# Six weight lows of the first expert on GpSimd during the choice of experts, six of the second expert's in their place on VectorE

## What is computed

```
logits = xn @ router_w + router_b
top_vals, top_idx = top_k(logits, 2)
h = relu(einsum('td,edh->eth', xf, w1) + b1)
y = einsum('eth,ehd->etd', h, w2) + b2
out = einsum('etd,te->td', y, gating)
x = x + s * silu(out)
```

## Time and profile before

| | |
|---|---|
| median of 3 runs | 1032.6 us (1032.31 to 1035.81) |
| the profiled execution | 1037.49 us, of which 1035.7 us are the span from first to last instruction |
| busy, share of the span | TensorE 94%, VectorE 84%, ScalarE 62%, GpSimd 33% |
| mean granted TensorE clock | 0.995 of full |
| routing and first two experts' lows | about 0 to 83 us |
| expert blocks on TensorE | from 78.4 us |

### The profile page before, as it was taken

One profiled execution on the slowest core, in us unless ns is written; L12 is line 12 of the kernel. 1 busy time (PEld: TensorE's weight loads), 2 busy tenths in 40 slices (PEclk: granted clock), 3 DMA queues, 4 the chain that ended last, 5 costly groups with the idle time before them and its releaser, 6 DMA issues.

```text
span 1035.7 us, 25206 instructions
## 1 busy us (share of the span) xinstructions
PE 978.3 (94%) x8418; PEld 764.4 (74%) x8418; DVE 875.0 (84%) x1707; ACT 646.0 (62%) x1383; POOL 338.6 (33%) x342
## 2 busy tenths in 40 slices
PE   0799999999999899999998999999999999999997
PEld 0667888888889799976666666776766777777786
DVE  7899889887676455659999999999999999999972
ACT  4853333333333243438898988888888888888860
POOL 2017889999996300011010102121212121212111
PEclk9999999999999999999999999999999999999999
DMA  9866776766665523227999999999999999999993
GB/s 284 257 268 156 192 195 181 201 191 185 179 180 168 149 57 63 68 87 151 186 169 183 164 178 176 187 196 169 177 187 180 197 187 182 174 168 172 169 179 99
DMA packets 426749, 178.39 MB, mean 172 GB/s; under 512 B 362714, under 2 KB 416548, under 8 KB 425860
## 3 DMA queue, kind: packets, MB, share of 16 engines
q1 hardware_dynamic: 364644, 131.53, 63.1%
q10 hardware_dynamic: 55504, 27.55, 10.5%
q0 software_dynamic: 6480, 17.70, 7.2%
HBM read 54.42 MB, written 34.60 MB: 86 GB/s over the span
## 4 chain that ended last, share of the span: by engine, by line
PE 37%; DVE 13%; issue 2%; ACT 2%; DMA 1%; ACTq 0%; SPq 0%; DVEq 0%
PE b_psS L1411 11%; PE b_psO L1439 11%; PE b_psJ L1456 6%; PE b_psJ L1370 5%; DVE b_ph L1652 4%; DVE b_nmax L1614 4%; PE b_psS L1467 2%; PE b_psO L1442 1%; DMA b_pT<-b_ph 1%; DVE b_outs L1658 1%; ACT b_pr L1521 1%; DVE b_psJ L1622 1%; DVE b_Q L1636 1%; ACT b_ph L1551 1%; DVE b_f L1664 0%
## 5 line engine op out<-in xcount | busy, mean ns | idle before, releaser
L1054 PE MATMUL psU<-bxT,w_p 128*128 128x256 f16 (+1 forms) x1920 | 285.6, 261 | 2.8 <-issue 1.3
L1152 ACT ACTIVATE h<-psU,bias 128x256 f32<-128x256 f32 (+1 forms) x320 | 126.7, 447 | 243.9 <-PE psU L1054 211.4
L1063 PE MATMUL psY<-w_p,hp 128*128 x1704 | 272.3, 273 | 2.5 <-issue 1.4
L1521 ACT ACTIVATE b_pr<-b_psS,b_nmax 128x1024 f32<-128x1024 f32 (+7 forms) x256 | 188.2, 743 | 58.3 <-DVE b_nmax L1612 36.2
L1411 PE MATMUL b_psS<-b_kp,b_Q 128*128 128x512 f16 (+3 forms) x1152 | 215.1, 326 | 3.1 <-PEq L1251 1.5
L1439 PE MATMUL b_psO<-b_pT,b_vp 128*128 128x256 f16 x1536 | 204.4, 274 | 8.4 <-DMA b_pT<-b_ph 3.4
L1054 PEld LDWEIGHTS psU<-bxT,w_p 128*128 x1920 | 188.0, 98 | 22.3 <-issue 5.5
L1652 DVE SCALAR_TENSOR_TENSOR b_ph<-b_pr,b_rrec,b_ph 128x1024 f16<-128x1024 f32 (+7 forms) x256 | 199.3, 811 | 1.9 <-ACT b_ph L1551 1.9
L1551 ACT ACTIVATE b_ph<-b_pr,b_rrec 128x1024 f16<-128x1024 f32 (+7 forms) x256 | 187.9, 779 | 0.0
L1063 PEld LDWEIGHTS psY<-w_p,hp 128*128 128x128 f16 x1704 | 166.8, 98 | 22.5 <-issue 2.6
L1179 DVE CAST hp<-h 128x512 f16<-128x512 f32 (+1 forms) x160 | 92.9, 581 | 101.3 <-ACT h L1152 99.5
(11 more groups left out here) (198 smaller groups left out, 1072.2 us busy)
## 6 DMA issues: line engine op xcount, KB each, us to landing
wstage<-in_L_ffn_w SPq DMA_DIRECT2D x48, 256.0 KB
expert_rows<-rowx SPq DMA_DIRECT2D x65, 128.0 KB
expert_outputs<-y ACTq DMA_DIRECT2D x31, 256.0 KB
b_pT<-b_ph SPq DMA_TRANSPOSE x320
a_x_all<-in_L_attn_x SPq DMA_DIRECT2D x8, 512.0 KB, 7.4
a_w_raw<-in_L_ffn_w SPq DMA_DIRECT2D x4, 1024.0 KB, 9.7
xn_split<-a_xp SPq DMA_DIRECT2D x4, 1024.0 KB, 8.9
xn_turned<-a_xT SPq DMA_DIRECT2D x3, 1024.0 KB, 15.9
```

The lines of the kernel that those rows point to most:

```text
L1054: mm = eng.matmul(psU[w % U][:, g % 2, 0:tiles * P].rearrange("p (t r) -> p t r", t=tiles), weight(n, a * W1 + c * H + g * P, P), bxT[n % ...
L1063: mm = eng.matmul(psY[n % 2][:, t, :], hp[n % 2][:, a, g, t * P:(t + 1) * P], weight(n, 2 * W1 + (2 * g + b) * D, D), start=(g == 0 and k ...
L1152: a = eng.activation(h32[w % 4][:, g, 0:rows], psU[w % U][:, g, 0:rows], ACT.Relu, bias=bias[:, ds(e * HT + 2 * q + g, 1)], scale=1.0 / WS)
L1521: a = eng.activation(pr[k % 3][:, o:o + w], psS[BUF[i]][:, :, :].rearrange("p a n -> p (a n)")[:, o:o + w], ACT.Exp, bias=nmax[:, at:at + ...
```

## The change

In `routing`, GpSimd makes the lows of pieces 2 to 7 before it waits for the stored rows and for `who`. It uses two instructions each, since it first scales the raw piece in place and then subtracts the high. VectorE waits for `w_done` of 8 behind `owners` and does pieces 8 to 13 where it did 2 to 7; pieces 14 and 15 remain at the start of `experts`.

```diff
+    ws0_ = whole.enter_context(nc.semaphore("first_scaled"))
...
+    def low_by_pool(eng, q):
+
+        hi, lo, _ = halves(q)
+        full = raw_of(q)
+        eng.wait_ge(wh0_, q + 1)
+        eng.tensor_scalar(full, full, WS, 1.0, ALU.mult, ALU.mult).then_inc(ws0_, 1)
+        eng.wait_ge(ws0_, q - 1)
+        eng.tensor_tensor(lo, full, hi, ALU.subtract).then_inc(wd_, 1)
...
         owners()
-        for q in range(2, PIECES):
+        eng.wait_ge(v["wd_"], PIECES)
+        for q in range(PIECES, 2 * PIECES - 2):
             v["first_low"](eng, q)
         eng.wait_ge(s_ft, 2)
...
             a.then_inc(s_xp, 1)
+        for q in range(2, PIECES):
+            v["low_by_pool"](eng, q)
         eng.wait_ge(xs_, 64)
...
-        for q in range(PIECES, FIRST):
+        for q in range(2 * PIECES - 2, FIRST):
             v["first_low"](eng, q)
```

## The result

The changed kernel takes 1044.66 us (median of 9 runs, 1039.97 to 1048.12), the kernel before beside it 1035.81 us (9 runs, 1032.31 to 1040.42). The ratio is 1.0094, with an interval of 1.0075 to 1.0113: **slower by 0.9%, some 9.7 us** (7.8 to 11.7), where 3.5 were forecast. A second set beside the experiments gave 1.009 (1.0062 to 1.0118).

The account below looks back on a forecast made before the run. It took the start of TensorE's expert blocks as the bound, set by VectorE's linked chain to the first one-hots, plus block 1's stalls. Sum: 1032.6 + 5.2 - 1.7 = 1036.1 us, range 1032.3 to 1039.8.

Parts of the forecast that it names:

- VectorE's lateness, +5.2: VectorE's chain before the first one-hots: waits for GpSimd's instructions make it 5.2 us late, bounds 0 and 7.4.
- The walk: Step through VectorE's chain, each engine waiting for the other's whole instruction, reductions and PSUM reads passing: 5.2 us late.
- Rivals 1 and 2: VectorE's chain: 1, GpSimd holds the port pair between instructions, 1038.3 us, chance 0.22; 2, lateness misses the path, 1030.9, 0.11.
- rival 3: VectorE's chain: only small instructions go without waiting, 3.4 us late, 1034.3 us; chance 0.15.
- rival 5: GpSimd is not finished by 73.7 us, so VectorE's new wait is real; no chance worth a number.
- The instruction that did not wait: A 16-column VectorE subtraction at 18.25 us, profiled before, ended at 18.51 while GpSimd ran on to 19.14.
- None is made good by the filling projections: TensorE's 30 projections before the first place were already done when the table came, so they absorb none of 5.2 us.
- The gain, -1.7: Block 1 on TensorE: stalls from late splits vanish as VectorE does fewer lows first, 1.7 us, bounds 0.8 and 1.8.
- the bound of 0.8: Lower bound, 0.8 us, of the 1.7 us expected from removing block 1's stalls.
- Rival 4, the clock: TensorE, idle from 49.84 us for up to 4 us longer, gets half-clock stretches, some 2 us more: 1038; chance 0.05.
- The sign of being wrong: Prediction is wrong if TensorE's shift at block 2 and the span's change differ by more than 1 us.
- Carrying one profiled execution over to the median: The profiled execution, 1037.49 us, is 4.9 above the median; the difference of 3.5 us was added to 1032.6.

Follow-up runs that it names:

- zeros: Changed kernel with GpSimd's six scalings and subtractions replaced by six memsets of the lows to zero; ratio to the kernel before 1.0004.
- scale_only: Changed kernel with GpSimd's six subtractions replaced by memsets to zero, the six scalings kept; ratio to the kernel before 1.005.
- fill: Changed kernel with 15 idle matmuls on TensorE ahead of the first place, results overwritten; ratio to the kernel before 1.0059, median 1041.88 us.
- late_chain: Kernel before with seven extra linked VectorE instructions ahead of the first one-hots, GpSimd idle; ratio to the kernel before 1.0098.
- fill5: Changed kernel with 5 idle matmuls on TensorE ahead of the first place; ratio to the kernel before 1.0057.
- three: Changed kernel with three pieces (2 to 4) on GpSimd instead of six, VectorE doing the others; ratio to the kernel before 1.0019.
- lead46: Changed kernel with 46 instead of 30 later key and value projections ahead of the first place; ratio to the kernel before 1.0091.
- mix: Kernel before with lows 12 to 15 behind block 0's first splits and gathers and stores of units 6 and 7 moved earlier; ratio 1.0001.

## Why the prediction was wrong

- **VectorE's lateness, +5.2.** Right in mechanism and nearly in size: 4.77 us, the size in part by luck. The walk missed where GpSimd's instructions met which of VectorE's (in the numbering of the changed kernel, the first L797, L794, L799 and L808 waited 0, 0.4, 0.3 and 0.1 us and not 0.6, 1.1, 0.8 and 0.8; L810 waited 0.6 and not 0.1; L820, L821 and L824, taken as free, waited 0.6, 0.4 and 1.0). All waits together are 5.35 us. Part of them is taken back, which the walk left out: the kernel before had 0.42 us of idle time there, ahead of L902, shown above. What the walk had wrong is the order: it put 4.4 of its 5.2 us ahead of the counts and 0.9 behind them, and the trace has 2.1 and 2.7. `zeros` and `scale_only` show that the lateness follows GpSimd's reads. Rivals 1 and 2 are out, and rival 3 as well: L803 (32 columns) and L824 (14) wait. So is rival 5: GpSimd is done at 57.47. What the Trainium skill says in "SBUF — State Buffer", section "Who interferes with whom", that two SBUF inputs contend with a GpSimd instruction that reads and not with one that only writes, agrees with both kernels (1.14 us for L803 beside reads, 0.42 for 256 columns beside memsets). The instruction that did not wait stays an exception that no run explained.
- **None is made good by the filling projections.** Right; TensorE's wait ahead of the first place grew from 0.55 to 3.27 us, which is less than the lateness only because the counts, ahead of the projections, came 2 us late themselves.
- **The gain, -1.7.** Of uncertain size. From the first `up` of block 0 to that of block 2 the changed kernel wins 2.1 and 0.8 us in its two traces; `zeros` wins 0.2 and `fill` loses 0.3. The lows were not the only thing between relu and `down`: GpSimd, let go sooner, takes its part back, as the bound of 0.8 allowed for. And a relu comes late: the second one of block 0 begins 3.2 us behind the block's start before, 2.9 in `late_chain`, 3.6 and 4.0 in the two traces of the changed kernel and 4.7 in `zeros`. The trace with the later relu has the smaller gain; that this is its cause was not tested.
- **Rival 4, the clock: the step that failed.** The sum has no term for the clock. As a rival it had a chance of 0.05 and a price of 2 us, with one stretch "near free" because the filling projections had slack. The fall was looked for in the wait for the choice, at 49.84. There it is free indeed (`fill5`). But the same lateness opens a second wait behind the projections, ahead of the first place. By the walk it would have been 0.55 + 0.9 = 1.45 us; since 2.7 us of the lateness came behind the counts, it was 3.27. And what follows there is the path itself: no slack, and work that left the clock down for 17.1 us instead of 3.4. That cost 4.15 us in the trace. The second trace of the changed kernel has the same, and the mean clock of all 15 executions, 0.987 to 0.991, fits it. `fill` takes the fall away and `late_chain` makes it without GpSimd, so it is shown that a late table on VectorE brings the half clock, and that filling the wait keeps it away. What it takes for a fall is not: `three` and `fill5` had it behind waits of 0.56 and 0.48 us, about as long as the 0.55 before.
- **The miss of 6.2 us, added up.** At block 2 the first trace has 4.77 + 4.15 - 2.1 = 6.8 us where the prediction had 5.2 - 1.7 = 3.5, and the second has 8.1. The clock is the larger part of the miss. The gain was larger than taken in one trace and smaller in the other. The 1.6 to 2.9 us between these shifts and the 9.7 of the ratio lie behind block 2 or between executions, and no run here locates them. The range ended at 1039.8, 7.2 us above 1032.6, and the interval of the measured difference begins at 7.8.
- **The sign of being wrong came.** TensorE's shift at block 2, 6.8 us, and the change of the span, 5.1, differ by more than 1 us: something later gives time back, and part of it are the two falls of the clock in the execution profiled before.
- **Carrying one profiled execution over to the median.** It was said that the difference carries over. It does not: the profiled executions differ by 5.1 us and the ratio says 9.7.

## What to carry to other kernels

An idle engine is not free when its reads hold what a linked chain on VectorE needs: twelve GpSimd instructions, 11.3 us of work, cost a chain of small VectorE instructions 4.8 us, and six memsets cost it nothing. When a change makes TensorE wait, look at each wait that it opens or widens, and at what TensorE does right behind it: a wait ahead of slack costs itself at most, a wait ahead of the critical path costs itself and, where the clock falls, the half clock after it (4.15 us here). Put real work into such a wait only if the place it is taken from does not become the next wait.

## What was not expected of the hardware

- The clock stayed at half for 13.7 to 20.5 us while TensorE was busy by the profile without a gap (16.90 of 16.90 us in the changed kernel), in the stretch of places of 71 columns between pairs of projections. In the six traces with such a fall (two of the changed kernel, `late_chain`, `scale_only`, `three`, `fill5`) it came back 2.2 to 3.0 us behind the end of the last place, in the unbroken row of projections. Falls elsewhere lasted 3.4 us, in `lead46` 6.8.
- At half clock the matmuls of 71 columns kept their pace (a place of 8 took 1.24 us, with 1.21 to 1.23 at full clock), and pairs of 512-column ones took 1.03 us instead of 0.61.
- The clock can fall without a long wait ahead: in the trace of `three` at 64.7 us, behind 0.56 us of idle time in the 11.6 us before (TensorE is busy 11.04 of them), in that of `fill5` at 67.0 us, and in 5 of 59 executions of the kernel before. What sets this was not tried.
- A memset of 128x512 float16 took 0.52 us and left VectorE's two-input instructions at 0.42 us.
- ScalarE's relus of block 0 came later than before with their input there: by some 1.3 us in `zeros` (the second), 2.6 us in `fill` and 4.4 us in `mix` (the first); the cause is open.
